# A GRU scan with expert layers: the input gates enter through TensorE, one sigmoid per unit reads the sum, and ScalarE makes 1-z

## What is computed

```python
def cell(h, x):
    gi = x @ W_ih + b_ih
    gh = h @ W_hh + b_hh
    i_r, i_z, i_n = jnp.split(gi, 3, axis=-1)
    h_r, h_z, h_n = jnp.split(gh, 3, axis=-1)
    r = jax.nn.sigmoid(i_r + h_r)
    z = jax.nn.sigmoid(i_z + h_z)
    n = jnp.tanh(i_n + r * h_n)
    h_new = (1.0 - z) * n + z * h
...
logits = flat_x @ Wg + bg                    # top 2 of 4 experts, softmax over them
for i in range(E):                           # 512 tokens per expert, D=512, H=2048
    h = jax.nn.gelu(tok @ W1[i], approximate=False)
    y = h @ W2[i] * p
    out = out.at[sel_idx].add(y)
```

## Time and profile before

| | us |
|---|---|
| median of 3 runs (lowest, highest) | 954.76 (952.18, 973.03) |
| profiled execution | 953.15 |
| its span, first to last instruction | 951.4 |
| TensorE busy | 798.6 (84%) |
| VectorE busy | 664.7 (70%) |
| ScalarE busy | 419.8 (44%) |
| GpSimd busy | 195.8 (21%) |

### The profile page before, as it was taken

How to read it: one execution, slowest core, us unless ns; L and a number is a source line. 1 busy time by engine, 2 the same in 40 slices (tenths; PEclk the granted TensorE clock), 3 DMA queues, 4 the chain that set the end, 5 groups by cost and what they waited for, 6 DMA issues and landing times.

```text
span 951.4 us, 27392 instructions
## 1 busy us (share of the span) xinstructions
PE 798.6 (84%) x11202; PEld 516.0 (54%) x11203; DVE 664.7 (70%) x2254; ACT 419.8 (44%) x844; POOL 195.8 (21%) x507
## 2 busy tenths in 40 slices
PE   6998788998888688887884514899999999999996
PEld 2444444577777677777774513444444444444442
DVE  5867777767888788888885586567765767575500
ACT  1656455654444344444442330574175418334700
POOL 1012111233333333333331001001201210210011
PEclk9999999999999999999997855999999999999999
DMA  9700000000000000000002274053525523370012
GB/s 346 273 2 2 1 2 2 2 3 3 4 3 4 2 4 3 4 3 4 4 3 90 91 221 165 14 180 85 167 61 171 154 67 132 90 208 12 1 18 27
DMA packets 20162, 62.52 MB, mean 66 GB/s; under 512 B 2064, under 2 KB 2064, under 8 KB 17424
## 3 DMA queue, kind: packets, MB, share of 16 engines
q1 hardware_dynamic: 15744, 52.46, 15.8%
q0 software_dynamic: 3584, 8.42, 5.0%
q10 hardware_dynamic: 720, 0.03, 0.0%
HBM read 52.49 MB, written 12.62 MB: 68 GB/s over the span
## 4 chain that ended last, share of the span: by engine, by line
PE 69%; DVE 20%; issue 5%; ACT 4%; DMA 1%; POOL 0%; DVEq 0%; POOLq 0%; SPq 0%; ACTq 0%
PE ps L344 21%; PE ps L486 17%; PE ps L499 17%; DVE wa L934 5%; PE ps L319 5%; DVE wa L939 4%; PE ps L336 3%; DVE wa L944 3%; DVE halves L955 3%; PE ps L428 2%; DVE ocand L948 2%; ACT wa L582 2%; PE ps L466 1%; DMA big<-in_w_ih 1%; PE ps L474 1%
## 5 line engine op out<-in xcount | busy, mean ns | idle before, releaser
L344 PE MATMUL ps<-halves,wa 128*128 128x64 f16 x8448 | 292.0, 194 | 76.6 <-DVE halves L955 66.4
L344 PEld LDWEIGHTS ps<-halves,wa 128*128 128x128 f16 x8448 | 272.2, 98 | 115.7 <-DVE wa L939 56.3
L582 ACT ACTIVATE wa<-wa,un_gates 128x128 f32<-128x128 f32 x288 | 112.6, 398 | 163.5 <-DVE wa L934 155.1
L486 PE MATMUL ps<-wb,big 128*128 128x512 f16 x768 | 166.9, 379 | 1.6 <-DVE wb L1246 1.6
L499 PE MATMUL ps<-big 128*128 128x512 f16 x768 | 166.9, 379 | 0.0
L486 PEld LDWEIGHTS ps<-wb,big 128*128 128x128 f16 x768 | 74.8, 98 | 91.6 <-issue 1.8
L587 ACT ACTIVATE wa<-wa,un_gates 128x64 f32<-128x64 f32 x288 | 94.1, 343 | 67.9 <-DVE wa L944 65.6
L499 PEld LDWEIGHTS ps<-big 128*128 128x128 f16 x768 | 75.2, 98 | 89.9
L934 DVE TENSOR_TENSOR wa<-ps,big 128x128 f32<-128x128 f32 x288 | 81.1, 287 | 54.0 <-PE ps L344 54.0
L336 PE MATMUL ps<-hx,wb 128*128 128x512 f16 x432 | 109.8, 386 | 0.0
L647 ACT ACTIVATE hx<-ps,un_hid_in 128x512 f32<-128x512 f32 x64 | 43.7, 683 | 112.5 <-PE ps L486 110.2
(11 more groups left out here) (168 smaller groups left out, 610.9 us busy)
## 6 DMA issues: line engine op xcount, KB each, us to landing
wa<-in_w SPq DMA_DIRECT2D x32, 1024.0 KB, 7.7
hs_rows<-big SPq DMA_DIRECT2D x8, 516.0 KB, 6.3
big<-in_w_ih SPq DMA_DIRECT2D x3, 1024.0 KB, 11.3
hx<-in_x_t SPq DMA_DIRECT2D x3, 1024.0 KB, 20.0
big<-in_w_hh SPq DMA_DIRECT2D x4, 768.0 KB, 16.4
wa<-in_x_t SPq DMA_DIRECT2D x1, 1024.0 KB, 4.9
hx<-hs_rows,idx POOLq DMA_INDIRECT x16
out<-hx,idx_out POOLq DMA_INDIRECT x16, 4.9
```

The lines of the kernel that those rows point to most:

```text
L344: mm = pe.matmul(gate_ps[:, j, g, :], whh_parts[:, k, w, (4 * g + j) * P:(4 * g + j + 1) * P], halves[:, src, k, h, :], start=(k == 0 and ...
L486: mm = pe.matmul(ps[:, m % 2, :], w1p[:, w, k, m * P:(m + 1) * P], tokT[:, t, k, :], start=(k == 0 and n == 0), stop=(k == KD - 1 and n == 2))
L582: act.activation(rz[:, j, :, :], pre[:, j, :, :], ACT.Sigmoid, scale=un_gates[:, 0:1]).then_inc(S["sig_done"], 1)
```

## The change

1. The r and z parts of `gi` are no longer stored in fp32. ScalarE keeps a tile in a ring of three (`gi_full`), scaled; then a HIGH and a LOW fp16 half are stored (`gi_rz`). For the first chunk ScalarE makes the HIGH half, for the others VectorE, in `between`/`other_work` at the end of its part of a step. VectorE makes all LOW halves.
2. TensorE adds them to the gates: a matmul of 128 columns with a scaled identity (`diag`) for each half and block (`inject`), two per block and exact step, one in a rough step. It is the first to write the bank. `pre_rz` is gone; `sig` reads PSUM.
3. ScalarE makes scale*(1-z) (`kept_of`), so `one_less_z`, `blend` and `keep_state` are plain two-input operations. `keep_pair` is gone: each block's state is kept alone, and in rough steps none is (the HIGH half is the state).
4. VectorE makes all four LOW halves; GpSimd only makes z*h.
5. `shift` is gone within the scan: in steps 7 and 39 `blend` and `keep_state` write to the neighbour's column, and `first_column` fills the first. It stays behind `check`.
6. The preparation also reduces the first chunk of `x`, and works out the scale of the biases and the two diagonals; the first tiles wait for that scale.
7. `ORDER` and the orders on VectorE and ScalarE are new, and the halves of W_hh are made in other steps (`WHH_AT`).

```diff
-        ORDER = ((HIGH, 0, 0), (HIGH, 1, 0), (HIGH, 2, 0), (HIGH, 3, 0), (HIGH, 1, 1), (HIGH, 3, 1),
...
+        ORDER = ((INJECT, 0, 0), (INJECT, 1, 0), (INJECT, 2, 0), (HIGH, 1, 0), (HIGH, 2, 0), (HIGH, 0, 0),
+                 (LOW, 0, 0), (HIGH, 1, 1), (LOW, 1, 0), (HIGH, 2, 1), (INJECT, 3, 0), (HIGH, 0, 1),
...
+        WHH_AT = {5: (0, 1), 6: (2, 3), 7: (4, 5), 8: (6, 7), 13: (8, 9), 14: (10,), 15: (11,)}
...
+            def inject(j, c, cols, parts, steps):
+
+                pe.wait_ge(S["rn_done"], steps + j + 1)
+                for part in parts:
+                    pe.matmul(gate_ps[:, j, 0:2, :], diag[:, 1 if c in (1, 2) else 0, :], gi_rz[:, c, j, part, :, cols],
+                              start=(part == HIGH), stop=False, skip_group_check=True)
...
+            pe.wait_ge(S["diag_ready"], 1)
             pe.wait_ge(S["whh_high"], KD)
...
                 def sig(j):
-                    act.wait_ge(S["pre_ready"], base + j + 1)
-                    act.activation(rz[:, j, :, :], pre[:, j, :, :], ACT.Sigmoid,
+                    act.wait_ge(S["gates_mm"], base + j + 1)
+                    act.activation(rz[:, j, :, :], gate_ps[:, j, 0:2, :], ACT.Sigmoid,
                                    scale=un_gates[:, 0:1]).then_inc(S["sig_done"], 1)
+
+                def kept_of(j):
+                    act.wait_ge(S["sig_done"], base + j + 1)
+                    act.activation(wz[:, j, :], rz[:, j, 1, :], ACT.Identity, bias=scale[:, STATE:STATE + 1],
+                                   scale=neg_scale[:, 0:1]).then_inc(S["wz_done"], 1)
...
+            dve.wait_ge(S["x_loaded"][0], 16)
+            dve.tensor_reduce(chunk_peak[:, 3:4], x_first, AX.XY, ALU.max, apply_absolute_value=True
+                              ).then_inc(S["chain"], 1)
...
-            for m in range(SCALED):
-                dve.wait_ge(S["gi_ready"], m + 1)
-                dve.tensor_scalar(gi[:, CHUNK_ORDER[0], m % 4, m // 4, :], gi[:, CHUNK_ORDER[0], m % 4, m // 4, :],
-                                  gates_scale[:, 0:1], None, ALU.mult).then_inc(S["first_scaled"], 1)
...
+                    dve.wait_ge(S["wz_done"], base + j + 1)
+                    dve.tensor_tensor(ocand[:, j, :], wz[:, j, :], cand[:, j, :], ALU.mult).then_inc(S["ocand_done"], 1)
...
+                exact = ((reset, 0), (candidate_in, 0), (reset, 1), (candidate_in, 1), (reset, 2),
+                         (one_less_z, 0), (candidate_in, 2), (blend, 0), (keep_state, 0), (one_less_z, 1),
+                         (low_part, 0), (blend, 1), (reset, 3), (candidate_in, 3), (one_less_z, 2),
+                         (keep_state, 1), (blend, 2), (low_part, 1), (one_less_z, 3), (keep_state, 2), (blend, 3),
+                         (keep_state, 3), (low_part, 2), (low_part, 3))
```

More of the change, by code:

```diff
@@ L344, in unit @@
                         mm = pe.matmul(gate_ps[:, j, g, :], whh_parts[:, k, w, (4 * g + j) * P:(4 * g + j + 1) * P],
-                                       halves[:, src, k, h, :], start=(k == 0 and g == 0 and h == HIGH and w == HIGH),
+                                       halves[:, src, k, h, :], start=False,
                                        stop=(stop and w == products[-1]), skip_group_check=True)
@@ L355, in gates_rough, with gates @@
                         if k == 0:
-                            pe.wait_ge(S["rn_done"], KD * i + j + 1)
+                            inject(j, *place(i), (HIGH,), KD * i)
                         unit(HIGH, j, k, src, (HIGH,), k == KD - 1)
-            def gates(src, base, low_base, steps):
-                seen, touched = set(), set()
+            def gates(src, c, cols, base, low_base, steps):
+                seen = set()
                 done = dict.fromkeys(range(KD), 0)
                 for h, j, k in ORDER:
-                    if j not in touched:
-                        pe.wait_ge(S["rn_done"], steps + j + 1)
-                        touched.add(j)
+                    if h == INJECT:
+                        inject(j, c, cols, (HIGH, LOW), steps)
+                        continue
                     if (h, k) not in seen:
@@ L980, in step, with first_column @@
-                for f, j in (exact if low else rough):
-                    f(j)
+                    dve.tensor_tensor(after(j), old(ocand_, j), old(zh_, j), ALU.add).then_inc(S["state_done"], 1)
+                def first_column(after_too):
+                    if after_too:
+                        link(dve.tensor_scalar(hs_s[:, :, 0, :, 0:1], h0[:, :, :].unsqueeze(3),
+                                               scale[:, STATE:STATE + 1], None, ALU.mult))
+                    link(dve.tensor_scalar(halves_s[:, dst, :, HIGH, :, 0:1], h0[:, :, :].unsqueeze(3),
+                                           scale[:, STATE:STATE + 1], None, ALU.mult))
@@ new lines, in other_work, with low_part @@
+                def other_work(j):
+                    for f, n in between:
+                        f(n)
+                def low_part(j):
+                    dve.wait_ge(S["state_done"], base + (j + 1 - KD * (ROUGH - 1)))
+                    whole = hs[:, j, 0, :] if moved else after(j)
+                    dve.tensor_tensor(halves[:, dst, j, LOW, :], whole, halves[:, dst, j, HIGH, :], ALU.subtract
+                                      ).then_inc(S["last_low_ready"], 1 + (POOL_LOWS if j == KD - 1 else 0))
@@ L982, in step, with shift @@
+                for n, (f, j) in enumerate(exact if low else rough):
+                    f(j)
+                    if moved and n == 0:
+                        first_column(low)
                 if low:
-                    last_low(KD - 1)
-            def shift(count, ends, starts, starts_all, low):
+                    other_work(0)
+            def shift(count, ends, starts, starts_all):
                 for k in range(KD):
@@ L1035, in _ @@
-                if s < KD and q < 2:
-                    x_low(q + 1, s)
-                if KD <= i < KD + WHH_PIECES:
-                    whh_low(i - KD)
+                between = []
+                if i < FILLED:
+                    for t in range(split_by(i - 1), split_by(i)):
+                        if TILES[t][1] < 8:
+                            between += [(rz_high, t), (rz_low, t)]
+                if 1 <= s <= KD and q < 2:
+                    between.append((x_low, (q + 1, s - 1)))
@@ L1040, in run @@
+                for n in WHH_AT.get(i, ()):
+                    between.append((whh_low, n))
+                step(lambda j, c=c, cols=cols: gi[:, c, j, 2, cols], after, i % 2, KD * i, i >= ROUGH - 1, moved, between)
             def run(steps):
```

329 lines of the change are left out of this document (188 added, 141 removed).

## The result

The changed kernel takes 917.25 us (median, 916.79 to 918.8) against 954.65 us for the kernel before on the same chip: a ratio of 0.9619, 95% interval 0.9597 to 0.9642. That is faster, 4 us above the forecast of 913. A step is counted from its first sigmoid to the next step's.

A forecast was written before the change was run, and what follows sets the result against it. It took TensorE's work to bound preparation and new rough steps, and the sigmoid-tanh-`blend` loop the exact steps. Terms -28 + 1.8 - 4 - 20 + 10.5 = -40 against 953.15 gave 913 us; range 901 to 926, with rivals 1 to 3 898 to 935.

The forecast's parts named there:

- Exact steps: Scan steps 24 on: the loop without the addition takes 5.25 us instead of 5.83; 48 steps give -28 us.
- rival 1: Exact steps: LOW half 3 comes later than TensorE needs it, steps stay near 5.7 us; 934 us in all; 10%.
- rival 2: Exact steps: GpSimd blocks VectorE on SBUF reads, 0.3 us per step; 928 us in all; 7%.
- Rough steps: Scan steps 0 to 19: TensorE's 5.50 us becomes the limit; 116 us instead of 136.4, -20 us.
- rival 3: ScalarE holds rough steps at 6.1 us and the preparation costs 14; 927 us in all; 7%.
- no idle time of 4 to 5 us: Sign that the prediction is right: no such TensorE idle time at steps 8 and 40.
- late by 0.5 to 1.6 us in six steps, about 4: Rough steps: VectorE's new halves of `gi` are not fully hidden, about 4 us within the 116.
- Steps 20 to 23: The four scan steps with 18 fills each: TensorE's own work, +0.45 us each, +1.8 us.
- Shift at step 40: Scan, step 40: TensorE's 5.06 us wait falls to 1.09, two linked operations add 0.5; net -4 us.
- Preparation: Before the scan: VectorE's queue delays the first fill by 9.7 us, a slow burst adds 1; together +10.5 us.
- The end: All behind step 71, the check and the expert layers: not touched by the change, 0 us.
- rival 4: Scan: changed rounding makes the check demand another 32 steps, 174 us more; 1087 us in all; 5%.

The follow-up runs named there:

- the execution of 3,012 us: One execution of the changed kernel with eight more 128-column matmuls per exact step from step 24; its other four took 915.7 to 918.7 us.
- the three orders: Changed kernel with reset/update tiles first, VectorE's preparation reordered, and new exact-step orders for TensorE's units, VectorE and ScalarE: 890.34 us, ratio 0.9342.

## Why the prediction was right, point by point

**The total is partly luck.** Term by term, measured less predicted is -2.9, +1.5, +3.0, +6.1, -1.0, -4.5 and +1.5 us: some 20 us of errors, of which 4 are left. The gaps at the starts of chunks, which the prediction did not foresee, were paid for in the main by exact steps that gained more than it said. Two slips in its working change nothing: 5.15 and 5.40 are -4.8 and +7.2 us over 48 steps and not -6 and +6, and its bounds simply added give about 898 to 932, where it takes 901 to 926 and doesn't say how.

**Exact steps: right, and undersold.** The loop ran as worked out: third sigmoid, tanh 0, `blend` 0, next burst, with 0.47 us of waits inside the burst where 0.4 were taken. The step is 5.15 against 5.25; the mean of all 46 went from 5.86 to 5.16 us, where 5.27 was taken, and so -32.5 against -28. The injections cost 0.056 us each, the straight line's value. The sigmoid takes 362 ns from PSUM; the experiment that feeds it from SBUF has 395. VectorE's tail, rival 1, did not bind: TensorE waits 0.11 us a step for LOW halves, where more than 0.3 would have been the sign. (The run with three of them on GpSimd doesn't settle it, since TensorE waits for those there.)

**GpSimd beside VectorE, rival 2: no.** In the changed kernel from 230 to 440 us, 39 of VectorE's two-input operations begin 0.06 to 0.08 us behind the start of a GpSimd operation and take 0.336 us (383.83 above is one); 40 begin 0.19 us behind one, inside it, and take 0.226, and the 643 that no GpSimd operation overlaps take 0.221. The price is 0.12 us once a step. The Trainium skill ("SBUF — State Buffer", Who interferes with whom) has the two contend for a port pair that it calls an exclusive lock. By that the operation at 383.83 would end at 384.31 or later, and its row ends at 384.17: the trace does not agree.

**Rough steps: the plain step right, the boundaries missed.** A plain rough step is 5.51 us, predicted 5.50, so 20 are 110.2, and ScalarE does not hold them (rival 3). The lateness of VectorE's halves was in the sum with 4 us, spread over six steps. It comes in one place a chunk (all the other rough steps take 5.45 to 5.51, but for the last, with 6.78, which hands over to the exact ones), for a cause that the prediction did not name: the first injection of a chunk wants all eight high halves, and the order of the tiles leaves two of them for VectorE's last minute. Steps 8 and 16 cost 7.9 us, step 24 7.5 us more, outside the term. The prediction said that no idle time of 4 to 5 us would be left at step 8; 3.46 were. The failed step is "late by 0.5 to 1.6 us in six steps, about 4": it counted VectorE's load, not who waits for which half first. With the other order of tiles the rough steps take 113.95.

**Steps 20 to 23.** Each interval of TensorE's own work is 8.53 us, as predicted (8.08 + 0.45). Of the +7.9, three of these intervals make 1.3, and the way to step 24 makes 6.5 (12.43 where 5.90 was).

**Shift at step 40: right.** 5.56 us remain of 10.60, with the two linked operations costing 0.4 (0.5 predicted).

**Preparation: mechanism right, size off both ways.** The queue is VectorE's, as said, and the run with another order shows it. The scale was there at 26.0, not 27.9: VectorE's wait for the all-reduce is 0.30 us now and was 1.44 in the earlier trace rows. The four LOW halves ended at 32.4 instead of 34.1, and all behind them was 2 to 3 us early, so the first fill came at 60.6 and not at 63.5. The idle time cost more than the 1 us: 13 fills took 5.67 us where the earlier trace rows has 2.97. In stretches of 2 us the granted clock is 0.50 (1.2 GHz) from 60.5 to 64.5, after 4.92 us of idling, and 1.00 from 66.5. The forecast was 2.9 too high in the one and 1.5 too low in the other, which leaves 1.4.

**The end** takes 1.5 us more; nothing of it is changed. Over the profiles of all kernels here, save the execution of 3,012 us, it lies between 445.2 and 448.0. What sets it was not looked into.

**Another 32 steps, rival 4:** they did not run: the page of the changed kernel has 8448 gate matmuls, 48 for each of 20 steps and 144 for each of 52.

## What to carry to other kernels

When a value is made ready ahead in several pieces, the new deadline is the first use that wants all of them: follow the last piece through its producer's queue, since the load of the producer doesn't show it. An engine that is 97% busy by the profile may have room: compare its sum of work with the step, or add work and see. Change the order of one engine's operations together with its neighbours', since an in-order queue can hold the old order against the new one; the kernel with the three orders, the tiles and the preparation put right takes 890.3 us, 27 less than the change alone.

## What had not been expected of the hardware

- A VectorE operation of 64 columns with two inputs in SBUF is longer beside GpSimd only when it begins in a certain window behind GpSimd's start: 0.336 us at 0.06 to 0.08 behind it, 0.344 at 0.09 to 0.10 and at 0.13 (the run with ScalarE's order alone, and the one with the sums copied out), 0.243 at 0.16 (the three orders), 0.226 at 0.19 and at 0.28. At 0.02 it mostly takes 0.22, as alone.
- An idle time of about 2.5 us may or may not cost TensorE its clock. After an idle 2.52 to 2.54 us, with the same wait ahead of them, the first fills ran at a clock of 0.50 to 0.70 in two kernels (13 fills in 4.67 us in each) and at 1.00 in a third (10 fills in 2.33 us); after 2.46 us at step 16 of the changed kernel it was 1.00. After 3.46, 4.92 and 5.41 us it was 0.52, 0.50 and 0.50.
